# A square-ReLU feed-forward kernel: the projection takes the rounded half of y first, x gets a second buffer, and two warm-up products go

## The reference

```python
q_emb = relu(cond @ W3 + b3)                                  # per batch
h0 = relu(((64 * x + sum of x over the 64 rows) * q_emb) @ W2 + b2)
w1, w2 = ternary(W_fc), ternary(W_proj)     # -s, 0 or +s; s is a group's mean |w|, groups of 64
h = square(relu(h0 @ w1.T))                                   # 2048 wide
out = x + (h * rsqrt(mean(h * h) + eps)) @ w2.T
```

## Time and profile before

| | before |
|---|---|
| median of three runs | 321.33 us (321.21 to 322.5) |
| the profiled execution, its time | 321.12 us |
| the same, span from first to last instruction | 319.1 us |
| PE busy | 313.4 us (98%) |
| DVE, ACT, POOL busy | 210.6, 192.1, 113.0 us |

### The profile page before, as it was taken

One profiled execution on the slowest core, in us unless ns is written; L12 is line 12 of the kernel. 1 busy time (PEld: TensorE's weight loads), 2 busy tenths in 40 slices (PEclk: granted clock), 3 DMA queues, 4 the chain that ended last, 5 costly groups with the idle time before them and its releaser, 6 DMA issues.

```text
span 319.1 us, 3835 instructions
## 1 busy us (share of the span) xinstructions
PE 313.4 (98%) x1326; PEld 238.8 (75%) x1326; DVE 210.6 (66%) x290; ACT 192.1 (60%) x282; POOL 113.0 (35%) x94
## 2 busy tenths in 40 slices
PE   8999999999999999999999999999999999999995
PEld 7664746545888788888888888888888888888884
DVE  0539989788888846676556655755655675665555
ACT  1658988799996884455544454644455554445550
POOL 1004333333733535413344431344433314433330
PEclk9999999999999999999999999999999999999999
DMA  6994959489521110016000000600000034000003
GB/s 190 358 279 111 286 138 291 108 191 275 73 49 34 33 36 1 0 46 219 0 0 2 0 0 0 244 23 0 0 2 0 0 116 149 0 0 2 0 1 133
DMA packets 31331, 27.02 MB, mean 85 GB/s; under 512 B 18736, under 2 KB 20816, under 8 KB 31312
## 3 DMA queue, kind: packets, MB, share of 16 engines
q1 hardware_dynamic: 29984, 26.25, 28.9%
q10 hardware_dynamic: 1328, 0.53, 0.7%
HBM read 18.39 MB, written 4.19 MB: 71 GB/s over the span
## 4 chain that ended last, share of the span: by engine, by line
PE 90%; ACT 4%; issue 3%; DVE 2%; POOL 0%; POOLq 0%; DVEq 0%; ACTq 0%
PE ps_out L320 34%; PE ps_acc L308 32%; PE ps_acc L292 17%; PE ps_out L273 5%; ACT x_t L568 1%; ACT x_t L565 1%; PE ps_acc L362 1%; DVE abs_sum L412 1%; DVE y_hi L452 1%; PE ps_x L377 1%; PE ps_acc L369 0%; ACT w_scale L532 0%; ACT w_t L545 0%; ACT w_abs L526 0%; PE ps_x L352 0%
## 5 line engine op out<-in xcount | busy, mean ns | idle before, releaser
L210 POOL TENSOR_TENSOR wv_sb<-wv_sb 128x512 f32<-128x512 f32 x55 | 82.2, 1494 | 114.1 <-ACT wv_sb L571 114.1
L320 PE MATMUL ps_out<-w_t,y_hi 128*128 128x512 f32 x256 | 101.7, 397 | 0.2 <-DVE y_lo L454 0.2
L320 PE MATMUL ps_out<-w_t,y_lo 128*128 128x512 f32 x256 | 101.0, 394 | 0.0
L308 PE MATMUL ps_acc<-h_hi,w_t 128*128 128x512 f32 x256 | 100.1, 391 | 0.0
L308 PE MATMUL ps_acc<-h_lo,w_t 128*128 128x512 f32 x256 | 100.0, 391 | 0.0
L454 DVE TENSOR_TENSOR y_lo<-x_t,y_hi 128x512 fp32r<-128x512 f32 x64 | 91.3, 1427 | 2.2
L565 ACT ACTIVATE x_t<-ps_acc 128x512 f32<-128x512 f32 x64 | 38.1, 595 | 81.1 <-PE ps_acc L308 81.0
L452 DVE CAST y_hi<-x_t 128x512 fp32r<-128x512 f32 x64 | 29.2, 457 | 73.6 <-PE ps_out L320 65.8
L320 PEld LDWEIGHTS ps_out<-w_t,y_hi 128*128 128x128 f32 x256 | 48.1, 188 | 11.5 <-DVE y_lo L454 0.6
L320 PEld LDWEIGHTS ps_out<-w_t,y_lo 128*128 128x128 f32 x256 | 48.4, 189 | 10.9
L308 PEld LDWEIGHTS ps_acc<-h_hi,w_t 128*128 128x128 f32 x256 | 48.3, 189 | 10.6 <-issue 0.2
(11 more groups left out here) (49 smaller groups left out, 147.5 us busy)
## 6 DMA issues: line engine op xcount, KB each, us to landing
x_sb<-in_x_dram SPq DMA_DIRECT2D x7, 1024.0 KB, 5.8
raw<-in_L_ffn_W_fc_dram SPq DMA_DIRECT2D x8, 512.0 KB, 5.3
raw<-in_L_ffn_W_proj_dram SPq DMA_DIRECT2D x8, 512.0 KB, 6.1
out_dram<-x_t SPq DMA_DIRECT2D x16, 256.0 KB, 2.1
x_sb<-in_x_dram SPq DMA_DIRECT2D x4, 256.0 KB, 5.5
wv_sb<-in_L_cond_W_dram SPq DMA_DIRECT2D x4, 256.0 KB, 7.1
x_t<-in_L_cond_W_dram ACTq DMA_DIRECT2D x1, 512.0 KB, 4.6
w_turned<-w_tern SPq DMA_TRANSPOSE x16, 3.1
```

Source lines behind the costliest of these rows:

```text
L210: engine.tensor_tensor(sq_acc[:], sq_acc[:], y_sq[:, v % SQ_RING, :], ALU.add).then_inc(sq_added, 1)
L308: last = pe.matmul(ps_acc[:, (UNITS + v) % ACC_RING, :], w_t[:, j, k * P:(k + 1) * P], part[:, k, g * BANK:(g + 1) * BANK], start=(k == 0 ...
L320: last = pe.matmul(ps_out[:, t, :], part[:, v % RING, t * P:(t + 1) * P], w, start=(j == 0 and part is y_hi), stop=(j == HJ - 1 and part i ...
```

## The change

Four edits. (1) `project` now issues the four products with `y_hi`, one for each row tile, behind a wait on `hi_done`, and then the four with `y_lo` behind the wait on `split`. The last tile of each group (j = 15) and the last two tiles of all keep the old order by row tile. In the opening tile of a group the waits on `finished` now stand before the four y_hi products. (2) x of odd groups is loaded into `x_odd`. It is allocated and released at once, so that `y_split`, which now holds both y_hi and y_lo and has the same size, lies on the same bytes. `load_x(g)` waits for the sums of group g-2, not g-1, and `load_x(1)` for nothing. (3) In SP's stream `load_x(1)` moves behind `load_wv(3)` and `load_pair(2)`, and `load_x(2)` and `load_x(3)` each move ahead by one turn. (4) The two warm-up products behind the transposes go.

```diff
-        y_hi = sb("y_hi", [P, RING, BANK], F32R)
-        y_lo = sb("y_lo", [P, RING, BANK], F32R)
+        with nc.sbuf_tensor("x_odd", [P, TT, D], F32) as x_odd:
+            pass
+        y_split = sb("y_split", [P, 2 * RING, BANK], F32R)
...
+        y_hi = y_split[:, 0:RING, :]
+        y_lo = y_split[:, RING:2 * RING, :]
+        x_of = [x_sb[:], x_odd[:]]
...
             def load_x(g):
-                sp.wait_ge(xt_done, KD * g)
-                sp.dma_start(x_sb[:], x_rows[g]).then_inc(x_loaded, 16)
+                wait(sp, xt_done, KD * (g - 1))
+                sp.dma_start(x_of[g % 2], x_rows[g]).then_inc(x_loaded[g % 2], 16)
...
                 if g == 0:
-                    sp.wait_ge(xt_done, KD * GROUPS)
+                    sp.wait_ge(xt_done, KD * (GROUPS - 1))
...
             load_wv(2)
-            load_x(1)
             load_wv(3)
             load_pair(2)
+            load_x(1)
             load_pair(3)
...
-                if i == 1:
+                if i == 0:
                     load_x(2)
-                if i == 4:
+                if i == 3:
                     load_x(3)
...
             def sum_x(g):
-                pe.wait_ge(x_loaded, 16 * g)
+                pe.wait_ge(x_loaded[g % 2], 16 * ((g + 1) // 2))
...
+            def project_part(v, t, part):
+                g, j = v // HJ, v % HJ
+                if j == 0 and part is y_hi:
+                    wait(pe, finished, TT * (g - 1) + t + 1)
+                return pe.matmul(ps_out[:, t, :], part[:, v % RING, t * P:(t + 1) * P], w_t[:, HJ + j, :],
+                                 start=(j == 0 and part is y_hi), stop=(j == HJ - 1 and part is y_lo))
...
             def project(v):
...
+                if j == HJ - 1:
+                    pe.wait_ge(split, v + 1)
+                    for t in range(TT):
+                        project_tile(v, t)
+                    return
+                pe.wait_ge(hi_done, v + 1)
+                for t in range(TT):
+                    project_part(v, t, y_hi)
                 pe.wait_ge(split, v + 1)
                 for t in range(TT):
-                    last = project_tile(v, t)
-                if j < HJ - 1:
-                    last.then_inc(projected, 1)
+                    last = project_part(v, t, y_lo)
+                last.then_inc(projected, 1)
...
-            for i in range(2):
-                pe.matmul(ps_acc[:, 1, 0:P], ident_f[:], ident_f[:], start=True, stop=True)
```

More of the change, by code:

```diff
@@ L152, in adaln_ffn @@
         x0_loaded = [sem(f"x0_loaded{t}") for t in range(TT)]
-        x_loaded = sem("x_loaded")
+        x_loaded = [sem(f"x_loaded{i}") for i in range(2)]
         res_loaded = sem("res_loaded")
@@ L271, in _, with sum_x_block @@
         def _(pe):
-            def sum_x_block(t, k):
-                return pe.matmul(ps_out[:, k, t * P:(t + 1) * P], x_sb[:, t, k * P:(k + 1) * P], sum_mat[:],
+            def sum_x_block(g, t, k):
+                return pe.matmul(ps_out[:, k, t * P:(t + 1) * P], x_of[g % 2][:, t, k * P:(k + 1) * P], sum_mat[:],
                                  start=True, stop=True)
             def sum_x(g):
-                pe.wait_ge(x_loaded, 16 * g)
+                pe.wait_ge(x_loaded[g % 2], 16 * ((g + 1) // 2))
                 pe.wait_ge(x1_ready, KD * g)
@@ L280, in sum_x @@
                     for t in range(TT):
-                        last = sum_x_block(t, k)
+                        last = sum_x_block(g, t, k)
                     last.then_inc(xt_done, 1)
@@ L311, in hidden @@
                 last.then_inc(hid_done, 1)
-            def project_tile(v, t):
[L314 to L322, removed]
+            def project_part(v, t, part):
[4 more added lines that the diff above has]
+                                 start=(j == 0 and part is y_hi), stop=(j == HJ - 1 and part is y_lo))
+            def project_tile(v, t):
+                project_part(v, t, y_hi)
+                last = project_part(v, t, y_lo)
+                if v % HJ == HJ - 1:
                     last.then_inc(tile_summed, 1)
-                return last
             def project(v):
@@ L381, in _ @@
                 for k in range(KD):
-                    last = sum_x_block(t, k)
+                    last = sum_x_block(0, t, k)
                     if t == TT - 1:
```

## The result

The changed kernel took 325.67 us (median of four executions, 325.14 to 326.36) against 321.27 us: a ratio of 1.0132, 95% interval 1.0102 to 1.0161, slower. The forecast was 323.5 us and slower; the measured median is 0.07 us above the upper end of the stated range (by the ratio, 321.33 x 1.0132 = 325.6, it is at that end). A ratio compares all executions of both kernels and not their medians, and so it can differ a little from the quotient of the medians. The profiled execution took 326.36 us, with a span of 324.3 us, 5.2 us more than before.

What follows compares the result with a forecast made beforehand. PE, with a product in flight for 98% of the span, was taken as the bound, so its stalls count in full. Terms -0.46 + 1.26 + 0.2 + 1.15 = +2.15 us on 321.33 gave 323.5 us, 8-in-10 range 321.4 to 325.6.

Steps and rivals of the forecast that it cites:

- Hi first where PE did wait: At 105 us, where DVE's y halves come late, PE's stall before the project goes: -0.46 us.
- Hi first at the openings: Opening projects of groups 1, 2 and 3: the fourth y_hi product waits for DVE's fourth finish, 3 x 0.42 = +1.26 us.
- Everywhere else: The 59 reordered projects: one more wait each, 0.2 us in all; doubled output bank changes put at nothing.
- Rivals 3, 4 and 6: 3: bank changes cost, 325.9, chance 0.08. 4: spacing closes, down to 315, 0.10. 6: bank cycling lowers clock, 340, 0.02.
- x of group 1: Its load, behind w_v and pair 2, lands at about 19.8 us, so PE's sums wait: +1.15 us.
- The two warm-up products: Dropping them at the start gains and costs 0; the wait for x would swallow up to 1.15 us.
- Rival 5: The clock falls to the lower level at PE's stall near 18.8 us, costing 1.5 us: 325.0 us, chance 0.05.
- the gaps in the openings: Sign: 0.4 us between third and fourth y_hi product in each of three opening projects, put down to DVE's L488.
- the 3.68 us between project starts: Sign: the distance of project starts stays at 3.68 us; anything else would mean the spacing was wrong.
- ACT without its wait for pair 2: Sign: ACT's wait for pair 2, 3.4 us before the change, is gone.
- The wait on the load into `x_odd`: Sign: PE or PEld waits 1.2 us near 18.8 us, at L273, on the DMA into x_odd.
- The likeliest case: Rival 1: both new waits and an unchanged spacing, 323.5 us, bounds 322.4 to 324.6, chance 0.56.

Runs made afterwards that it cites:

- e3: The kernel before with only the projections in the new hi-first order, opening tiles included: 321.95 us, ratio 1.0025.
- e6: The kernel before with the new order in the projections, except each group's opening tile in the old order: 320.78 us, ratio 0.9983.
- e5: The changed kernel itself, run again unaltered: nine executions at 322.32 to 322.68 us, three at 326.02 to 326.29.
- e4: The kernel before with only x_odd, y_split and the new order of the loads: 321.75 us, ratio 1.0016.
- e12: The kernel before with x_odd and the new load order alone, but x of group 1 ahead of pair 2: 320.95 us, ratio 0.9988.
- e1: The changed kernel with the two warm-up products put back behind the transposes: 322.46 us, ratio 1.0043.
- e8: The changed kernel with the two products placed between the sums of row tiles 0 and 1 of the first group: 322.42 us, seven executions.
- e9: The changed kernel with seven warm-up products at the head instead of five, none behind the transposes: 322.34 us, eight executions.
- e2: The kernel before without the two warm-up products, nothing else changed: six executions at 320.69 to 321.65 us, six at 325.18 to 325.66.
- e7: The changed kernel with warm-up products back, opening tiles in the old order, and x of group 1 loaded ahead of pair 2: 320.73 us, ratio 0.9979.
- e11: The changed kernel with old-order opening tiles, x ahead of pair 2, and four warm-up products behind the transposes: 320.60 us, ratio 0.9982.
- e10: The changed kernel with three warm-up products at the head instead of five: two executions at 322.47 and 322.51 us, five at 325.46 to 326.22.

## Why the prediction was right or wrong

**The direction was right, and so were the places of the two new waits; most of the measured size came from a step that I had put at nothing.** Step by step:

- *Hi first where PE did wait*: forecast -0.46. Right in place and kind. The profiles give -0.56, since the three hidden tiles behind the old stall took some 0.03 us more than 1.82 each and do so no more.
- *Hi first at the openings*: forecast 3 x 0.42 = 1.26, between the third and fourth product. Measured 0.40, 0.43 and 0.39, there; taking the opening tiles out of the new order gives 1.2 to 1.7 us back (e3 against e6, by the way in which two series are compared).
- *Everywhere else*: forecast 0.2 for the waits and nothing for the bank changes. Nothing for both. Rivals 3, 4 and 6, which needed another pace, are out. The Trainium skill, TensorE: Matmul & The Clock Gate, tells under "A second HAM failure mode: psum-queue depth-cycling" of idle times between groups of products when banks are cycled; here the banks change twice as often as before, no such idle time is seen, and the pace is the same to 0.01 us in eight products.
- *x of group 1*: forecast to land at 19.8, +1.15. It landed at 10.38 + 8.9 = 19.3, and the wait is worth +0.54 (e5's profile) to +0.65 (e4). The order of the queue was read rightly, which e12 shows by turning one pair of loads around; the time at which the last of it is through was read 0.5 us too late, and this term was mis-sized by half.
- *The two warm-up products*: this is the step that failed. The prediction put them at 0, with "The same wait would swallow up to 1.15 us if the clock rose later for the missing products". The clock did rise later, in 7 of 16 executions by their times, and in the profiled one not by a little but by 10 us. It held PE back by 4.37 us up to the sums of group 1, and the wait for x could swallow no more than its own 0.54. What is left in such an execution is 3.7 us (median of the seven, 326.08) on top of the 322.4 of an early one. Rival 5 had the clock, but put the danger at 18.8 us, behind PE's stall there, with 1.5 us. No fall there was seen.

Of the signs that the prediction names, the gaps in the openings, the missing gap at 105 us, the 3.68 us between project starts and ACT without its wait for pair 2 came as forecast. The wait on the load into `x_odd` is there in e5's profile, half as long, and not in the profile of the first measurement.

Without the late clock the change costs some 0.8 to 1.4 us against the medians of the same series (e1 +1.36; e5's early executions and e8 +0.8; e9 +1.2), and 1.2 by e5's profile. That is within what I took to be no difference, and my sum of 2.15 was about 1 us too high: 0.61 in the wait for x, 0.2 in the waits of the 59 projects, 0.1 at 105 us. The measured 4.4 us is this and the late clock, which all four executions of the first measurement had. The likeliest case's own range, 322.4 to 324.6, holds the early kind at its lower edge and not the late one. So it was luck that the verdict came out "slower", and near the end of the range: four early executions would have given about 322.4, under the 322.9 from which I called it slower. What carried the result over that bound is not in the sum.

What the runs show of the late rise: it comes when the two products are taken away, from either kernel (e2, e5). It stays away with them in their old place, at the head, or in the gap before row tile 1 (e1, e9, e8: no execution at 325 or more in 20, nor any in e3, e4, e6, e7, e11 and e12, which have them in the old place). With yet two fewer it comes in five of seven (e10), too few to tell that share from 7 of 16. So that the two products keep it away is shown, and that they need not stand in their old place. *How* they do it is not. One reading is that it is their number. The other is the gap: with them, PE has work without a break until the x of row tile 1 is there, also at the lower level (the two tiles' sums are one run of 16 records in the profiles of the kernel before and of e9, with the rise at 6.9 and 7.0 us, and e8 fills the gap). Without them, PE stands still for 0.42 us just before 6.8 us in the late profile, and for 0.57 in e10's, while in the early profiles of e2 and e5 the clock was up before the gap. No run separates the two readings; five products with x of row tile 1 landing earlier, or seven with the gap left open, would. Why one execution of the same program is early and the next late, the runs don't show either, and the share differs between occasions: four of four, then three of 12. The Trainium skill, TensorE: Matmul & The Clock Gate, says under "What's actually happening" that the same kernel meets a different number of slow products from run to run, and that the rise costs under 1% of a typical kernel's span; the runs agree with the first, and not with the second, at 3.7 us of 322.4, 1.1%.

## What to carry to other kernels

A product that computes nothing may be what brings TensorE's clock up in time. Before one is dropped because it "only fills a wait", it has to be priced with the clock rising late, and the kernel has to be run often enough to see two kinds of execution: four executions of one kind made this change look like 4.4 us, and the median of mixed ones describes neither.

When products are regrouped, follow every wait that moves with them: the hi-first order put the wait for the last of four finishes three products earlier, and that alone made a gain of 0.56 us into a loss of 0.66 by the profiles' terms, 0.85 by the medians. With the opening tiles left in the old order, the products back, and x ahead of pair 2 in the queue, the change so mended is a little faster than the kernel before, at a ratio of 0.9979 (0.9968 to 0.9990).

Where a queue has work all the time, as here from 7 us on, a load that is issued earlier lands no earlier than the bytes ahead of it let it: x, issued 1.25 us earlier but behind two more loads, landed at 19.3 instead of 17.2 us. What decides is its place, here half a megabyte (e4 against e12).

## What the hardware showed that was not expected

SP's issues themselves can stand still. SP's timeline of the changed kernel:

```profile
5.35 3.54 SPq L231 DMA_DIRECT2D wv_sb<-in_L_cond_W_dram  x2
8.93 1.41 SPq L221 DMA_DIRECT2D raw<-in_L_ffn_W_proj_dram  x1
10.38 0.68 SPq L236 DMA_DIRECT2D x_odd<-in_x_dram  x1
```

In the kernel before these issues take some half a microsecond each. Here the two of w_v, issued one behind the other, took 3.54 us and that of pair 2 took 1.41, so that x was issued at 10.38, a mere 1.25 us before its old 11.63. In e1, e4, e5, e7 and e12 the two of w_v take 3.0 to 3.4 us as well. Earlier loads were still under way; that their number holds the issue up is a guess.

TensorE stayed at its lower level for 10.3 us in which its records followed each other without a gap, from 6.81 to 17.1 us. Of the other profiles only that of e10 is like it (sums of group 1 at 23.35 us); in all the rest PE began these sums between 18.5 and 20.1 us. By the distance of the records the clock rose at 5.0 to 7.0 us in eleven profiles, at 9.2 in that of e8, and at 17.1 and 17.5 in the two late ones. With no execution of the changed kernel between 322.7 and 325.1 us, the late rise looks like another kind of start and not like the tail of a spread.
